# A two-layer graph network: swapping the z sums and the pre-activations in a step of the second layer

## The reference

```python
edge_index = jnp.stack([src, dst])
h = jnp.maximum(_layernorm(x, axis=-1), 0.0)
x = x + _L0_gnn_ref(h, L0_gnn_weight, src, dst, edge_type_16)
h = jnp.maximum(_layernorm(x, axis=-1), 0.0)
x = x + _L1_gnn_ref(h, edge_index, edge_attr_8, W1, b1, W2, b2)
```

```python
msg_input = jnp.concatenate([x[src], x[dst], edge_attr], axis=1)
h = jax.nn.relu(msg_input @ W1 + b1)
msg = h @ W2 + b2
out = jax.ops.segment_sum(msg, dst, num_segments=x.shape[0])
```

## Time and profile before

| what | value |
|---|---|
| median of 3 runs | 5686.32 us (5675.06 to 5697.63) |
| the profiled execution's own time | 5690.92 us |
| its span, first to last instruction | 5689.2 us |
| TensorE busy, share of the span | 51% |
| GpSimd busy, share of the span | 55% |
| VectorE and ScalarE busy | 23% and 13% |
| mean granted TensorE clock | 0.673 |

### The profile page before, as it was taken

How to read it: one execution, slowest core, us unless ns; L and a number is a source line. 1 busy time by engine, 2 the same in 40 slices (tenths; PEclk the granted TensorE clock), 3 DMA queues, 4 the chain that set the end, 5 groups by cost and what they waited for, 6 DMA issues and landing times.

```text
span 5689.2 us, 67280 instructions
## 1 busy us (share of the span) xinstructions
PE 2886.9 (51%) x21226; PEld 2230.5 (39%) x21226; DVE 1335.7 (23%) x2704; ACT 720.5 (13%) x1391; POOL 3156.5 (55%) x3343
## 2 busy tenths in 40 slices
PE   1455555555454554555535545545545555554455
PEld 1343433344343443443424433433434334443334
DVE  5222222223232322322421111111111111111111
ACT  2000110101101101101111111111111111111111
POOL 5555555555555555555355555555555555555554
PEclk9666666666666666666756666666666666666666
DMA  3111111111111111111011111111111111111111
GB/s 83 21 21 26 24 21 26 24 21 25 25 22 26 24 22 26 24 22 26 19 29 27 29 27 28 27 28 28 27 29 28 26 29 29 26 29 28 25 30 25
DMA packets 239638, 153.83 MB, mean 27 GB/s; under 512 B 177657, under 2 KB 177705, under 8 KB 239267
## 3 DMA queue, kind: packets, MB, share of 16 engines
q0 software_dynamic: 106496, 109.26, 10.2%
q1 hardware_dynamic: 130129, 39.04, 3.2%
q10 hardware_dynamic: 2642, 0.63, 0.1%
HBM read 133.39 MB, written 14.45 MB: 26 GB/s over the span
## 4 chain that ended last, share of the span: by engine, by line
PE 40%; issue 38%; another core or an unknown queue 14%; DVE 5%; SPq 2%; DVEq 1%; ACT 1%; DMA 0%; ACTq 0%
PE ps L1185 9%; PE ps L1123 8%; PE ps L1132 7%; PE ps L1177 5%; PE ps L1167 4%; PE ps L1174 4%; DVE onehot L934 2%; DVE acc L992 2%; SPq L517 1%; PE ps L1155 1%; PE ps L1106 1%; PE ps L1165 1%; DVEq L992 1%; DVEq L985 0%
## 5 line engine op out<-in xcount | busy, mean ns | idle before, releaser
L633 POOL DMA_INDIRECT rows<-p_table,idx x1664 | 1569.7, 943 | 1293.6 <-DMA idx<-in_src_dram 737.5
L633 POOL DMA_INDIRECT rows<-h_table,idx x1616 | 1532.6, 948 | 1180.0 <-DMA idx<-src_tab 693.7
L1123 PE MATMUL ps<-onehot,rows 128*64 128x128 f32 x6656 | 807.5, 339 | 832.2 <-issue 748.6
L1123 PEld LDWEIGHTS ps<-onehot,rows 128*64 128x64 f32 x6656 | 565.3, 170 | 1048.5 <-issue 945.7
L1132 PE MATMUL ps<-slots,w_pairs 128*64 128x128 f32 x3328 | 597.4, 329 | 358.5 <-issue 349.1
L1177 PE MATMUL ps<-q_win,onehot_t 128*128 128x64 bf16 x4992 | 333.7, 209 | 841.6 <-issue 840.5
L1177 PEld LDWEIGHTS ps<-q_win,onehot_t 128*128 128x128 bf16 x4992 | 255.5, 108 | 1072.7 <-issue 1072.3
L1132 PEld LDWEIGHTS ps<-slots,w_pairs 128*64 128x64 f32 x3328 | 497.4, 171 | 435.6 <-issue 415.2
L992 DVE TENSOR_TENSOR acc<-acc,ps 64x16 f32 x1664 | 272.4, 164 | 1678.0 <-remote 1143.4
L1185 PE MATMUL ps<-onehot,relus 128*65 128x128 f32 x3328 | 585.1, 333 | 159.3 <-issue 155.4
L1185 PEld LDWEIGHTS ps<-onehot,relus 128*65 128x65 f32 x3328 | 490.5, 174 | 201.2 <-issue 197.4
(11 more groups left out here) (103 smaller groups left out, 760.0 us busy)
## 6 DMA issues: line engine op xcount, KB each, us to landing
rows<-p_table,idx POOLq DMA_INDIRECT x1664
rows<-h_table,idx POOLq DMA_INDIRECT x1616
q_win<-q_table SPq DMA_DIRECT2D x208, 48.0 KB
attr<-in_edge_attr_dram SPq DMA_DIRECT2D x209, 32.0 KB
q_table<-q SPq DMA_DIRECT2D x12, 360.0 KB
idx<-in_src_dram SPq DMA_DIRECT2D x208, 4.0 KB
idx<-src_tab SPq DMA_DIRECT2D x202, 4.0 KB
xs<-in_x_dram SPq DMA_DIRECT2D x6, 480.0 KB, 11.9
```

The costliest lines, as they stand in the source:

```text
L633: pool.indirect_dma_start(rows[:, u, t, :], None, table, bass.IndirectOffsetOnAxis(ap=idx[:, u, t:t + 1], axis=0)).then_inc(s, 16)
L1123: last = pe.matmul(slot_ps[par * D:(par + 1) * D, b, t, :], rows[:, u, t, :], onehot[:, b, t, par * C0:(par + 1) * C0], start=True, stop=True)
```

## The change

Only the order of two pairs of calls in each step of the second layer is changed, on TensorE and on VectorE, with the same swap in the steps behind the loops. TensorE's step becomes turn (k), z sums (k-2), pre-activation (k-1). VectorE's step becomes one-hot (k+1), window (k-2), rows (k-1). Each wait moves with its call. SyncE's, GpSimd's and ScalarE's programs stay as they are.

```diff
@@ -1040,10 +1040,10 @@
                 def step(it, u, first=False):
                     k = it * U + u
                     make_onehot1(k + 1, (u + 1) % 4)
+                    if not first or u >= 2:
+                        add_window(k - 2, u % 2)
                     if not first or u >= 1:
                         add_rows(k - 1, it if u else it - 1, (u - 1) % U)
-                    if not first or u >= 2:
-                        add_window(k - 2, u % 2)
@@ -1051,8 +1051,8 @@
                 segments(dve, step, chunk_out, begin=1)
+                add_window(G - 2, G % 2)
                 add_rows(G - 1, NIT - 1, U - 1)
-                add_window(G - 2, G % 2)
                 add_window(G - 1, (G - 1) % 2)
@@ -1188,16 +1188,16 @@
                 def step(it, u, first=False):
                     k = it * U + u
                     turn_group(k, it, u)
+                    if not first or u >= 2:
+                        sum_group(k - 2, (u - 2) % U)
                     if not first or u >= 1:
                         products(k - 1, it if u else it - 1, (u - 1) % U)
-                    if not first or u >= 2:
-                        sum_group(k - 2, (u - 2) % U)
@@
                 segments(pe, step, chunk_out, begin=1)
+                sum_group(G - 2, U - 2)
                 products(G - 1, NIT - 1, U - 1)
-                sum_group(G - 2, U - 2)
                 sum_group(G - 1, U - 1)
```

## The result

The changed kernel takes 5708.92 us at the median of 20 runs (5681.54 to 5730.59), the kernel before in the same comparison 5686.36 us. The ratio is 1.0036 with a 95% interval of 1.0020 to 1.0051: slower, by 22.6 us, and less than the 0.5% that I had called a change. I had forecast 134 us. The time itself lies in the stated range.

A forecast was written before the change was run, and what follows sets the result against it. Bound: a two-group cycle, 20 us of gathers then some 7 us without, set by SyncE's next signal and TensorE's remaining work. 62 + 75 + 30 - 35 = 132 us on 5690.9, against the median about 5820 us; range 5645 to 5990.

The forecast's parts named there:

- Step (b): TensorE when the relu ends late under gathers: z sums and products left until after them; 75 us, bounds nothing to 475.
- The sign that I had named for (b): Idleness before line 1185 ended by ScalarE's relu rises from 1 us to a hundred or more; idleness before 1177 falls.
- what I had said would show me wrong: Line 1185 waits for relus and the second layer's stage still lasts 2735 us, so something else bounds.
- Step (a): TensorE in quiet steps: transposes cover 0.98 of the relu's 1.55 us; about 0.6 us exposed 104 times, 62 us.
- Step (c): SyncE's next idx load starts late after the products' late signal, delaying GpSimd's restart; 30 us, bounds nothing to 121.
- Step (d): The twelve output chunks: ScalarE's copy can be made while products run; gain 35 us, between nothing and 116 us.
- The rival "no change": Same instructions go through the same slow passage under gathers, or SyncE's list or GpSimd bounds; 5686 us, chance 0.15.
- The rival "faster": TensorE's z sums pass under gathers, products run in the open; 5538 us, 5628 if in half the cycles; chance 0.15.

The follow-up runs named there:

- idx2_after: The changed kernel with SyncE loading idx two groups ahead; 5723.24 us, ratio 1.0111 to the kernel before.
- pe_only: The kernel before with only TensorE's half of the swap, VectorE's order kept; 5705.98 us, ratio 1.0035.
- p1_before: The kernel before with only one of the three bf16 parts multiplied in line 1177; 5582.75 us, ratio 0.9852.
- lat4_after: The changed kernel with the relu made four times in a row; 5864.45 us, ratio 1.0369 to the kernel before.
- the control: The kernel before, in its old order, with the relu made four times in a row; 5655.52 us, ratio 0.9999.

## Why the prediction was wrong

The direction was right and the mechanism was seen; the size was 5.8 times too large (132 us in the sum, 22.6 measured).

**Step (b), the steps whose relu is late, is the one that failed.** I took 75 us with an upper bound of 475, for a P that ends later. It compared the end of one P in both orders (0.8 us left after the gathers before, S and P afterwards) and charged the difference. But the old order has its S, of the group before, still to do directly behind that P: 3.66 us at 4186.63 in the earlier trace rows. In the new order that S is done ahead of its P. S moved from behind one P to ahead of the next, and was not added. Nor did P's signals come late more often: VectorE's waits for late ones at line 1031 fell from 1111 us in 101 times to 857 us in 90. The sign that I had named for (b) did appear, 606 us more of waiting on line 1185, 537 of them ended by a relu, but without its price: 441 us came back in line 1177 and 138 us in lines 1167, 1174 and 1155, 41 us were added in line 1165, and TensorE's idleness in all rose by only 69 us. This is nearly what I had said would show me wrong, a line 1185 that waits for relus in a stage that lasts as long as before (29 us more by the count of groups).

**Step (a), quiet steps, had the right price and too many places.** The price is right: 4.97 against 4.32 us, and with one gather a group the swap costs 168 us, 135 of them at this price. With all gathers, (a) to (c) together come to 22.6 us if the chunks gave nothing, and to 22.6 + 40 = 63 us if they gave the whole 40 us below; I had 167. The run with a second relu says the same: 0.69 us a step uncovered, 24 us in all under gathers. The cases I had counted as open, one in each pair, are mostly not: in the trace after, of the 79 waits for a relu on line 1185 only 28 are shorter than 1 us, 16 us together, for the 104 times 0.6 us that I took. How the cost that is left divides over (a), (b) and (c) no run here separates.

**Step (c), what is late next.** GpSimd's mean wait for idx did not rise towards 8 us, it fell from 7.0 to 6.7 with eight more waits. These are 24 us more in all, but that doesn't confirm the 30 I took: GpSimd issues the same gathers in either kernel, so any lengthening of the stage shows up as its waiting. What changed is the number of runs of gathers, 102 before and 108 after in 2980 to 5650, 26 of them of one group's eight where there were 13; the stretches between them are not longer. Why there are more, no run shows. `idx2_after` shows that loading idx earlier doesn't help, so the delay that I drew from P's signal through SyncE to the restart is not the bound.

**Step (d), the chunks, held as idleness and is not shown as time.** Line 1155's idleness fell from 116.0 to 76.1 us, 40 us for the 35 taken. But `pe_only`, where the window addition still stands behind the rows, keeps 114.1 us of it and takes the same time as the whole change. Unless VectorE's half costs as much elsewhere, these 40 us were not on the path.

**The clock** was in no term. The mean granted clock rose from 0.673 to 0.685, yet a matmul of line 1185 took 361 ns in the mean where it had taken 335. What this is worth in the 22.6 us no run separates; with one gather a group the two clocks are alike, 0.753 and 0.755, and the swap costs its full price.

The rival "no change" came out, by half of its mechanism. That the same instructions go through the same slow passage is right. That SyncE or GpSimd alone bounds the stage is not: with all eight gathers, fewer matmuls do shorten the kernel (`p1_before`), relus that come later lengthen it (`lat4_after`), and an earlier idx load does not shorten it. A supply of instructions that is slow whatever GpSimd does is out, since the gaps vanish with the gathers while TensorE's program and its loops stay; one that the gathers slow down is not excluded. The rival "faster", z sums hidden under gathers, didn't come about; that the relu is late too often for it is my reading, which no run tests.

The picture that fits the runs is a sum, roughly. The second layer takes TensorE's plain step, 4.3 us a group, and on top most of the time in which GpSimd issues gathers: 2735 - 208 x 4.32 = 1836 us, where 208 x 8 gathers at 1.25 us from one to the next take 2080. What TensorE waits for late in a run of gathers is free, what it waits for outside is paid. The sum alone, with 4.97 for 4.32 us, would charge the swap 135 us; it costs 23 because most of the new waits fall where TensorE crawls. In the old order relus could be 2 us later in either kind of stretch at no cost, as the control shows.

## What to carry to other kernels

Before a stall is charged to a change, ask what the engine gets done in that stretch now: a wait that fills a stretch in which the engine crawls is free, and the test is to take the crowding away (here most of the gathers) and see whether the full price appears. When a block is moved, compare the whole work between two fixed points and not one block's end, or the moved block is counted twice. A line whose idle time is the largest, and an engine that waits for a load again and again, can both be symptoms: here 441 us left one line for another, and an earlier load gained nothing.

## What the runs showed of the hardware

Each gather instruction holds GpSimd for 0.94 us, with 0.30 us to the next. From one to four a group the kernel takes, by the ratios, (0.8046 - 0.6882) x 5686 / 3 / 208 = 1.06 us more for each, from four to eight (1 - 0.8046) x 5686 / 4 / 208 = 1.34 us, though TensorE reads nothing in this layer that the gathers write. While gathers are issued, a semaphore of TensorE can arrive 14.4 us late (P through at 4176.87, VectorE and SyncE going on at 4191.26 and 4191.29), bf16 matmuls go singly with 1.9 us between them, and with one gather a group line 1177 has no idle time at all. It takes some microseconds of gathers to set in: in the earlier trace rows they start at 4163.02, and a whole P still goes in 0.86 us at 4165.19. Through which part of the chip the gathers do this, no run here shows.
